# Sparse experts in a fused two-layer kernel: tokens sorted by expert in two halves, the first half's sorting placed inside the last attention iterations, and the order tables rewritten

## The chip, the cores and the metric

The kernel runs on one core of one Trainium2 chip. The metric is the device time of one execution in microseconds (us). A profiled execution also has a span: the time from its first to its last recorded instruction. TensorE is called PE, VectorE DVE, ScalarE ACT, GpSimd POOL; SyncE (SP) issues the DMAs.

## The reference, cut to what matters

Two layers run on 4 batches of 256 tokens with 128 channels (1,024 tokens) and a context of 512 rows for each batch. Layer 0 is cross-attention with 8 heads of 64 and a feed-forward with a quantized piecewise-linear GELU. Layer 1 is cross-attention with 16 heads of 8, with a small ReLU block, and then a mixture of 8 experts of which each token takes its best two:

```python
def _L1_ffn_ref(x, Wg, W1, W2, W3):
    t = x.reshape(-1, D)                      # 1024 x 128
    probs = jax.nn.softmax(t @ Wg, axis=-1)   # 8 experts
    top_v, top_i = jax.lax.top_k(probs, TOP_K)          # TOP_K = 2
    top_v = top_v / (jnp.sum(top_v, axis=-1, keepdims=True) + 1e-08)
    comb = jnp.zeros((T, E), dtype=t.dtype).at[jnp.arange(T)[:, None], top_i].add(top_v)
    out = jnp.zeros_like(t)
    for e in range(E):
        h = jax.nn.silu(t @ W1[e]) * (t @ W3[e])        # 128 -> 512
        out = out + comb[:, e:e + 1] * (h @ W2[e])      # 512 -> 128
    return out.reshape(Bb, Ll, D)
...
    x = x + _L1_ffn_ref(_layernorm(x, axis=-1), L1_ffn_Wg, L1_ffn_W1, L1_ffn_W2, L1_ffn_W3)
```

## The kernel before, in words

**Order of work.** One function, `schedule()`, writes a single list of steps, and each engine walks the same list and does its own share of each step (`for kind, *at in order`). The attention part of the list comes from eight iterations, one for each layer and batch (0 to 3 are layer 0, 4 to 7 are layer 1). Every step has a place inside its iteration, counted in heads; the places stand in the tables `PLACES` (a default for each layer) and `SHIFTED` (values for one iteration), and the list is sorted by them. The engines meet only in semaphores, so a wait on one engine holds back everything behind it in that engine's part of the list.

**Attention.** For each head PE computes scores twice: once for the row maxima (`maxima`, L468, reduced by DVE in L766) and once transposed (`scores`, L498), whose exponential ACT takes from PSUM (L1056). `attend` (L530 in layer 1) multiplies by the values. In layer 1 an iteration has 16 heads; maxima of the next batch are taken one iteration ahead, so iteration 7 needs none of its own. Layer 0's feed-forward and layer 1's projections of earlier batches stand between the heads. POOL splits the 24 expert weight blocks into a high and a low float16 part in iterations 4 to 7 (`split`, L1212 and L1213); SP loads them (`stage_in`, L1314).

**Experts.** After the last head the list has 2 halves x 8 experts x 4 chunks of 128 hidden units. A half is 512 tokens, and every expert is computed for all of them. For a chunk PE does six matmuls of 512 columns (`gate_up`, L653: up and gate, each as high x high, high x low and low x high), ACT takes the SiLU (L1122), DVE the product (L953), ACT and DVE split it into a high and a low part (L1129, L958). For each expert `down` (L670; `down_last`, L684, for the final one) does 48 matmuls of 128 columns, and DVE's `mix` (L968) adds each result to `x_sb` with the token's share `comb`, which is zero for the six experts that the token doesn't take. Shares come from `logits`, `route` (with an exponential written as a power on POOL, L1204), `shares`, `compare`, `rank` and `best`. The list `rest` puts those steps, and the last batch's projections, between the chunks. At the end SP writes each half of the output in one DMA (L1339).

**PSUM.** `p_misc` has four banks used in turn (`misc_take`, `misc_wait`, `misc_done`); in the expert part two of them hold the up product and the other two stay in turn. `p_sc` holds the gate product and `p_o` the down product.

Of the kernel before, what the change touches and what calls it, by code (L numbers as in the profile page):

```python
# [8 lines left out]
F16 = mybir.dt.float16  # L9
AX_X = mybir.AxisListType.X  # L10
# [20 lines left out]
VW = DH1 + 1  # L31

# [3 lines left out]
    0: {"max": (1.5, 1.0), "sum": 1.38, "av": (-0.38, 0.96), "f_ln": -0.65, "f_xn": 0.92, "f_xT": 1.2,  # L36
        "up0": (1.4, 0.13), "round": 1.57, "floor": 2.0, "nodes": 2.17, "slope": 3.0, "interp": 3.5, "ident": 3.7,
# [17 lines left out]
    (2, 'f_ln'): 0.02, (2, 'interp'): 3.48, (2, 'q1'): 5.66, (2, 'slope'): 2.71, (2, 'sum'): 2.35,  # L55
    (2, 'v0'): (3.6, 1.02), (3, 'av'): (-0.45, 0.96), (3, 'nodes'): 2.58, (3, 'oT'): (5.14, 0.71), (3, 'sT'): 3.68,
    (3, 'v1'): 5.23, (4, 'av'): (0.05, 1.0), (4, 'bounce'): 12.04, (4, 'down0'): 7.55, (4, 'f_ln'): 1.46,
    (4, 'f_xT'): 2.5, (4, 'f_xn'): 2.1, (4, 'floor'): 3.9, (4, 'ident'): 6.9, (4, 'interp'): 6.3,
    (4, 'nodes'): 4.19, (4, 'oT'): (5.0, 1.99), (4, 'round'): 3.55, (4, 'rows'): 2.08, (4, 'slope'): 5.5,
# [3 lines left out]


def schedule():
# [27 lines left out]
    for it in range(2 * B):  # L93
# [10 lines left out]
        if nxt:  # L104
            put(it, 1.7 if it == 0 else -0.01, "stack0" if nxt[0] == 0 else "stack1", nxt[1])
# [68 lines left out]
        if it == 2 * B - 1:  # L174
            put(it, 0, "split", 3 * E - 1)
            for i in range(2):
                tokens(lambda name, n, *what: step(name, *what, n=n), i, i)
            step("route", "route", 0)
# [4 lines left out]
    rest = {0: [("oT1", B - 1, 0)], 1: [("oT1", B - 1, 1)], 2: [("shares", 0)], 3: [("compare", 0)], 4: [("rank", 0)], 5: [("best", 0)],  # L183
            6: [("aT1", B - 1)], 8: [("h1", B - 1)], 10: [("y1", B - 1)]}
    for i, b in enumerate((2, 3)):
        for chunk, kind in ((11, "ln"), (13, "xn"), (15, "xT")):
            rest[chunk + 5 * i] = rest.get(chunk + 5 * i, []) + [(kind, "ex", b)]
        rest[17 + 5 * i] = [("logits", b)]
    rest.update({24: [("route", 1)], 28: [("shares", 1)], 30: [("compare", 1)], 34: [("rank", 1)], 36: [("best", 1)]})
    for n in range(2 * E):  # L190
        for f in range(FF):
            order.append(("gu", n, f))
            if n and f >= 2:
                order.extend([("dn", n - 1, 2 * (f - 2)), ("dn", n - 1, 2 * (f - 2) + 1)])
            order.append(("act", n, f))
            order.extend(rest.get(FF * n + f, []))

    order += [("dn_last", f) for f in range(FF - 1)] + [("act", 2 * E, 0), ("dn_last", FF - 1), ("mix", 2 * E - 1)]
# [28 lines left out]
def build(nc, t, out):  # L227
    ctx = ExitStack()
    with ctx:
# [39 lines left out]
        ew = [region[:, 8192 * i:8192 * (i + 1)].rearrange("p (s e n) -> p s e n", s=2, e=E) for i in range(3)]  # L269
# [15 lines left out]
        xh = qS[:, 0, 0:8, :].rearrange("p h n -> p (h n)").rearrange("p (s n) -> p s n", s=2)  # L285
        cmp_ = kS[:, 0, 0:4, :].rearrange("p h n -> p (h n)").bitcast(F32).rearrange("p (s t e f) -> p s t e f", s=2, t=B * T, e=E)
# [6 lines left out]
        euler = sb("euler", [P, 1])  # L293
# [23 lines left out]
        hh = probs[:, 2:6, :].bitcast(F16).rearrange("p (b s) (f n) -> p b s f n", b=2, f=FF)  # L317
# [5 lines left out]

        dk = nc.dram_tensor("k_scratch", (B, 3, P, C), F16).ap()
# [67 lines left out]
        def _(pe):  # L392
# [44 lines left out]
            def xt(kind, b):  # L437
                n = norms.index((kind, b))
                pe.wait_ge(ln_xn, n + 1)
                transposes(("xT", kind, b), [xn[:, n % 2, i, :] for i in range(T)])  # L440
# [259 lines left out]
        def _(dve):  # L700
# [271 lines left out]
            def activate(n, f):  # L972
# [3 lines left out]
                if k:  # L976
                    low(k - 1)
# [393 lines left out]
```

## Time and profile before

| | us |
|---|---|
| median of 3 runs (lowest, highest) | 501.96 (501.45, 503.52) |
| the profiled execution | 501.99 |
| its span | 500.3 |
| PE busy in the span | 436.3 (87%) |
| DVE busy | 367.7 (73%) |
| ACT busy | 266.2 (53%) |
| POOL busy | 176.6 (35%) |
| mean granted clock of TensorE | 0.939 of full speed |

Busy time of PE is modelled from the size of each matmul and includes overlap of matmuls that are in the pipe together, so a group of matmuls is costed below by the distance between the starts of groups, not by the duration of one. The share of busy time is a mean over stages with different limits, and the stages must be read one by one.

### The profile page before, as it was taken

The numbers are of one execution on the slowest core, as the hardware profiler recorded it, in microseconds if no ns is written. First come the engines' busy times: TensorE is split into PE (matmuls) and PEld (weight loads), VectorE is DVE, ScalarE is ACT, GpSimd is POOL, SyncE is SP. The second block draws the span as 40 slices with busy tenths as digits, with TensorE's granted clock in tenths as the row PEclk, the third lists the DMA queues.
The fourth block names the chain that finished last, engine by engine and source line by source line (L and its number), as shares of the span: only waits on it lengthen the run. The fifth ranks groups of instructions, "written<-read, shape, count | busy, mean of one in ns | idle before, by whom it ended". The sixth has DMA issues, their size and how long they took to land.

```text
span 500.3 us, 8970 instructions
## 1 busy us (share of the span) xinstructions
PE 436.3 (87%) x3344; PEld 248.6 (50%) x3344; DVE 367.7 (73%) x718; ACT 266.2 (53%) x504; POOL 176.6 (35%) x205
## 2 busy tenths in 40 slices
PE   8569498997789968977985899999989999999996
PEld 3315154564356436544542544545546665656555
DVE  6855354555875799869986999882298888987775
ACT  3515253653824552456567376678755646465553
POOL 4218935427463492752426035710400104000000
PEclk9958698998979979997998899999999999999999
DMA  6664408007102005321142015400000000000000
GB/s 165 151 150 95 94 2 189 1 1 173 49 1 64 2 0 139 94 72 55 54 128 84 2 48 144 115 2 1 2 0 1 1 3 1 1 21 2 1 1 22
DMA packets 31487, 26.70 MB, mean 53 GB/s; under 512 B 4717, under 2 KB 28461, under 8 KB 31149
## 3 DMA queue, kind: packets, MB, share of 16 engines
q1 hardware_dynamic: 31445, 26.13, 20.9%
q8 instruction: 27, 0.44, 0.4%
q14 instruction: 15, 0.12, 0.1%
HBM read 12.10 MB, written 2.88 MB: 30 GB/s over the span
## 4 chain that ended last, share of the span: by engine, by line
PE 59%; DVE 22%; ACT 7%; issue 4%; SPq 3%; DMA 2%; POOL 2%; DVEq 0%; ACTq 0%; POOLq 0%
PE p_o L670 7%; PE p_sc L498 7%; PE p_misc L653 7%; PE p_sc L653 6%; PE p_misc L468 6%; DVE mx L766 6%; PE p_o L530 5%; PE p_o L517 4%; PE p_misc L399 4%; SPq L1254 3%; DVE xn L729 2%; DVE probs L953 2%; PE p_misc L425 2%; PE p_misc L562 2%; ACT probs L1122 2%
## 5 line engine op out<-in xcount | busy, mean ns | idle before, releaser
L766 DVE TENSOR_REDUCE mx<-p_misc 128x1 f32<-128x512 f32 x192 | 122.3, 684 | 20.4 <-PE p_misc L468 18.8
L1056 ACT ACTIVATE probs<-p_sc 128x512 f32<-128x512 f32 x192 | 104.6, 596 | 57.2 <-PE p_sc L498 56.9
L1122 ACT ACTIVATE probs<-p_misc 128x512 f32<-128x512 f32 x64 | 38.1, 597 | 56.6 <-PE p_sc L653 56.6
L953 DVE TENSOR_TENSOR probs<-probs,p_sc 128x512 f32<-128x512 f32 x64 | 44.0, 687 | 26.5 <-ACT probs L1122 24.7
L653 PE MATMUL p_misc<-qS,region 128*128 128x512 f16 x192 | 52.0, 380 | 3.8 <-DVE probs L953 2.6
L653 PE MATMUL p_sc<-qS,region 128*128 128x512 f16 x192 | 51.9, 379 | 0.0
L468 PE MATMUL p_misc<-kS,qS 96*128 96x512 f16 x128 | 40.6, 395 | 8.1 <-DVE mx L766 4.1
L1195 POOL TENSOR_TENSOR psums<-probs 128x256 f32<-128x256 f32 x32 | 26.0, 812 | 58.6 <-PE p_o L524 56.1
L1153 POOL TENSOR_SCALAR veps<-meanvar 128x2 f32<-128x2 f32 x16 | 3.7, 230 | 121.7 <-DVE meanvar L718 121.3
L670 PEld LDWEIGHTS p_o<-region,probs 128*128 128x128 f16 x720 | 42.7, 98 | 7.1
L670 PE MATMUL p_o<-region,probs 128*128 128x128 f16 x720 | 45.1, 219 | 0.0
L517 PE MATMUL p_o<-probs,v 128*64 128x256 f32 x256 | 38.3, 423 | 7.0 <-ACT probs L1056 7.0
L498 PE MATMUL p_sc<-qS,kS 128*128 128x256 f16 x256 | 40.6, 278 | 4.2 <-ACT probs L1056 3.9
L958 DVE TENSOR_TENSOR probs<-probs 128x512 f16<-128x512 f32 x64 | 43.8, 684 | 0.0
L530 PE MATMUL p_o<-probs,v 128*32 128x256 f32 x512 | 41.0, 398 | 0.0
L1129 ACT CAST probs<-probs 128x512 f16<-128x512 f32 x64 | 39.1, 611 | 1.4 <-DVE probs L953 1.4
L498 PE MATMUL p_sc<-region 128*128 128x256 f16 x256 | 36.6, 290 | 0.9 <-DVE region L780 0.9
L498 PEld LDWEIGHTS p_sc<-qS,kS 128*128 128x128 f16 x256 | 23.4, 98 | 19.8 <-ACT probs L1056 8.0
L498 PEld LDWEIGHTS p_sc<-region 128*128 128x128 f16 x256 | 25.7, 103 | 12.6 <-issue 3.6
L1213 POOL TENSOR_TENSOR region<-v,region 128x512 f16<-128x512 f32 x24 | 30.3, 1264 | 1.9
L653 PEld LDWEIGHTS p_sc<-qS,region 128*128 128x128 f16 x192 | 18.8, 98 | 22.7
L517 PEld LDWEIGHTS p_o<-probs,v 128*64 128x64 f32 x256 | 16.8, 146 | 24.7 <-issue 12.7
(163 smaller groups left out, 678.6 us busy)
## 6 DMA issues: line engine op xcount, KB each, us to landing
region<-kx SPq DMA_DIRECT2D x24, 256.0 KB, 3.9
v<-in_L_ffn_W_dram SPq DMA_DIRECT2D x24, 256.0 KB, 2.7
region<-qx SPq DMA_DIRECT2D x24, 128.0 KB, 3.9
kS<-kS SPq DMA_DIRECT2D x1, 1664.0 KB
kS<-k_scratch SPq DMA_DIRECT2D x8, 192.0 KB
k_scratch<-kx SPq DMA_DIRECT2D x4, 256.0 KB, 2.2
qS<-q_scratch SPq DMA_DIRECT2D x8, 96.0 KB
probs<-in_ctx_dram SPq DMA_DIRECT2D x1, 576.0 KB, 6.2
```

The lines of the kernel that those rows point to most:

```text
L468: pe.matmul(ps, q[:, i * P:(i + 1) * P], k, start=True, stop=True).then_inc(full, 1)
L498: last = pe.matmul(p_sc[:, half, j * S:(j + 1) * S], k[:, kt * P:(kt + 1) * P], q, start=(i == 0), stop=(i == len(pairs) - 1))
L517: pe.matmul(p_o[64 * i:64 * i + 64, 0, m * S:(m + 1) * S], v0[:, b % 2, kt, h * DH0:(h + 1) * DH0], probs[:, h % 8, kt * S:(kt + 1) * S], ...
L530: last = pe.matmul(p_o[32 * j:32 * j + 32, n % 2, 0:S], v1[:, b % 2, c, h * VW:h * VW + 32], probs[:, h % 8, c * S:(c + 1) * S], start=(c ...
L653: last = pe.matmul(ps[:, f % 2, :], w[:, ws, e, f * P:(f + 1) * P], xh[:, xs, half * C:(half + 1) * C], start=(i == 0), stop=(i == 2))
L670: last = pe.matmul(p_o[:, n % 2, i * P:(i + 1) * P], hh[:, n % 2, hs, f, i * P:(i + 1) * P], ew[2][:, ws, e, f * P:(f + 1) * P], start=(at ...
L766: dve.tensor_reduce(mx[:, b % 2, i, h:h + 1], ps, AX_X, ALU.max).then_inc(free, 1)
L953: dve.tensor_tensor(hp[:, k % 2, :], sg[:, k % 2, :], p_sc[:, k % 2, :], ALU.mult).then_inc(hp_done, 1)
L958: dve.tensor_tensor(hh[:, n % 2, 1, f, :], hp[:, k % 2, :], hh[:, n % 2, 0, f, :], ALU.subtract).then_inc(hl_done, 1)
L1056: act.activation(probs[:, h % 8, half * 512:(half + 1) * 512], p_sc[:, half, :], ACT.Exp, scale=(DH0 if layer == 0 else DH1) ** -0.5).then ...
L1122: act.activation(sg[:, k % 2, :], p_misc[:, k % 2, :], ACT.Silu).then_inc(sg_done, 1)
L1129: act.copy(hh[:, last_n % 2, 0, last_f, :], hp[:, (k - 1) % 2, :]).then_inc(hh_done, 1)
```

## The change

The expert part no longer computes every expert for every token. The tokens of a half (512, each with two experts) are sorted by expert into slots of 128 rows. Each expert gets as many slots as its tokens need, rounded up; 15 slots (`SLOTS`) always suffice for a half, and all 15 are computed. For each half:

- DVE marks each token's two experts (`mask`, at the end of `rank`); PE counts them with eight small matmuls (`count`); DVE works out each token's two row numbers, each slot's expert and the shares (`place`).
- POOL writes the normalized tokens (`xe`) into DRAM at their row numbers with eight indirect DMAs (`send`); SP reads the sorted rows back with four DMAs (`fetch`); PE transposes them slot by slot and ACT and DVE split them (`taken_t`, steps `gT`).
- For each slot PE reads the slot's expert number into a register (`value_load`) and addresses the weights by it: six matmuls of 512 columns, four transposes of the product, then four matmuls of 256 and four of 128 columns. The result goes to DRAM (`keep`).
- POOL gathers each token's two results with eight indirect DMAs (`pick`), DVE adds them to `x_sb` (`mix`) and SP writes the output in four DMAs for a half (`store`).

The first half's sorting (`ex` steps of batches 0 and 1, `route` to `send`, `fetch`, `gT`) now has places in iterations 6 and 7; the second half's stands between slots 0 and 18 of the first (`REST`). Both DRAM buffers are filled with zeros once (`wipe`, 2 DMAs in iteration 3). The POOL power is replaced by an exponential on ACT. The tables `PLACES` and `SHIFTED` are rewritten for all iterations; among others, the maxima of the last batch now start at place 3.42 of iteration 6 and stand 1.26 apart (2.62 and 1.01 before), so that heads 10 to 15 fall into iteration 7.

```diff
+NT = B * T // 2
+SLOTS = 2 * NT + E - 1
+GROUPS = -(-SLOTS // 4)
...
+    (6, 'max'): (3.42, 1.26), (6, 'nodes'): 0.12, (6, 'oT'): (6.04, 2.2), (6, 'oT1'): (4.48, 0.24),
...
+REST = [(0.12, 'oT1', 3, 0), (0.72, 'oT1', 3, 1), (1.17, 'aT1', 3), (1.4, 'h1', 3), (1.55, 'y1', 3),
+        (1.93, 'ln', 'ex', 3), (2.05, 'xn', 'ex', 3), (3.06, 'xT', 'ex', 3), (3.27, 'logits', 3),
+        (3.29, 'route', 1), (3.51, 'shares', 1), (3.63, 'compare', 1), (3.68, 'rank', 1), (4.61, 'best', 1),
+        (4.79, 'count', 1), (4.84, 'place', 1), (5.44, 'send', 1), (8.85, 'fetch', 1), (11.76, 'gT', 1, 0),
+        (13.86, 'gT', 1, 1), (17.72, 'gT', 1, 2), (18.76, 'gT', 1, 3), (19.42, 'pick', 0), (20.61, 'mix', 0, 0),
+        (21.99, 'mix', 0, 1), (26.65, 'mix', 0, 2), (31.47, 'mix', 0, 3)]
...
+            for name in ("route", "shares", "compare", "rank", "best", "count", "place", "send", "fetch"):
+                step(name, name, 0)
+            for q in range(GROUPS):
+                step("gT", "gT", 0, q, n=q)
...
+    for k in range(2 * SLOTS):
+        placed += [(k, ("gu", k)), (k + 1.3, ("hT", k)), (k + 2.6, ("dn", k))]
+    placed += [(at, tuple(what)) for at, *what in REST]
+    order += [what for at, what in sorted(placed, key=lambda step: step[0])]
+    order += [("pick", 1)] + [("mix", 1, i) for i in range(NT)]
...
+            def gate_up(k):
+
+                half, j = k // SLOTS, k % SLOTS
+                if j == 0:
+                    pe.wait_ge(experts_set, half + 1)
+                misc_done(pe, ("gT", half, j // 4))
+                chosen[k] = pe.value_load(expert_id[0:1, half, j:j + 1], min_val=0, max_val=E - 1)
                 if k == 0:
+                    pe.wait_ge(stage_free, 3 * E)
...
                 for ps, w in ((p_misc, ew[0]), (p_sc, ew[1])):
                     for i, (ws, xs) in enumerate(((0, 0), (0, 1), (1, 0))):
+                        last = pe.matmul(ps[:, k % 2, :], takenT[half][:, xs, at], w[:, bass.ds(chosen[k], 1), ws, :].rearrange("p e n -> p (e n)"),
                                          start=(i == 0), stop=(i == 2))
                 last.then_inc(gu_full, 1)
...
+            def hidden_t(k):
+                pe.wait_ge(hp_done, k + 1)
...
+                for f in range(FF):
+                    last = pe.transpose(p_o[:, k % 2, f * P:(f + 1) * P], hp[:, k % 2, f * P:(f + 1) * P], ident[:, :])
+                last.then_inc(hT_full, 1)
+
+            def down(k):
+                pe.wait_ge(hl_done, k + 1)
+                ps, full = misc_take(pe, ("ym", k))
+                for f in range(FF):
+                    w = ew2[:, bass.ds(chosen[k], 1), f, :, :].rearrange("p e s n -> p (e s n)")
+                    pe.matmul(ps[:, 0:2 * P], hh[:, k % 2, 0, f * P:(f + 1) * P], w, start=(f == 0), stop=False)
+                for f in range(FF):
+                    w = ew2[:, bass.ds(chosen[k], 1), f, 0, :].rearrange("p e n -> p (e n)")
+                    last = pe.matmul(ps[:, 0:P], hh[:, k % 2, 1, f * P:(f + 1) * P], w, start=False, stop=(f == FF - 1))
+                last.then_inc(full, 1)
...
+            def send(half):
+
+                pool.wait_ge(slots_set, half + 1)
...
+                for i in range(NT):
+                    for s in range(2):
+                        pool.indirect_dma_start(d_in[half], bass.IndirectOffsetOnAxis(ap=slot_id[:, half, s, i:i + 1], axis=0),
+                                                xe[:, half * NT + i, :], None).then_inc(sent, 16)
...
+            def fetch(half):
+
+                sp.wait_ge(sent, 16 * 2 * NT * (half + 1))
...
+            def keep(k):
+                misc_done(sp, ("ym", k))
+                sp.dma_start(d_out[k // SLOTS].rearrange("(t p) n -> p t n", p=P)[:, k % SLOTS, :], y_sb[:, k % 4, :]).then_inc(y_kept[k % 4], 16)
```

## Rows read from the trace of the kernel before

**Rows 1.** Busy time of each engine by stretch; last columns: granted clock, DMA share, GB/s.
```profile
core 0: us, PE busy (x) PEld busy (x) DVE busy (x) ACT busy (x) POOL busy (x), PEclk, DMA share, GB/s
...
250.00:298.50 48.50, 39.51 (x314) 20.02 (x312) 41.94 (x76) 29.44 (x58) 16.27 (x18) 0.93 0.23 66
298.50:328.50 30.00, 30.00 (x276) 15.33 (x278) 26.22 (x48) 20.83 (x45) 17.83 (x20) 1.00 0.43 112
328.50:357.10 28.60, 27.65 (x268) 13.44 (x272) 13.67 (x35) 23.71 (x51) 1.87 (x4) 1.00 0.01 1
...
359.40:389.27 29.87, 27.26 (x207) 16.06 (x203) 23.47 (x62) 17.26 (x32) 4.71 (x3) 1.00 0.00 1
...
414.43:487.78 73.35, 72.30 (x648) 44.50 (x649) 59.49 (x130) 39.80 (x73) 5.42 (x1) 1.00 0.02 5
496.37:500.30 3.93, 0.01 (x1) 0.00 (x0) 1.13 (x4) 0.00 (x0) 0.00 (x0) 1.00 0.23 67
```

**Rows 2.** The chain that ended last: experts of the expert part, and its end.
```profile
414.43 0.82 PE p_misc L653 x3
...
422.58 0.82 PE p_misc L653 x3
...
430.73 0.82 PE p_misc L653 x3
...
495.53 0.86 PE p_o L684 x12
```

**Rows 3.** Groups of instructions from 380 us on: busy us, mean ns, idle before.
```profile
L958 DVE TENSOR_TENSOR probs<-probs 128x512 f16<-128x512 f32 x56 | 38.3, 684 | 0.0
...
L1129 ACT CAST probs<-probs 128x512 f16<-128x512 f32 x56 | 34.2, 611 | 0.4 <-DVE probs L953 0.4
L1122 ACT ACTIVATE probs<-p_misc 128x512 f32<-128x512 f32 x55 | 32.9, 597 | 50.9 <-PE p_sc L653 50.9
L968 DVE SCALAR_TENSOR_TENSOR x_sb<-p_o,comb,x_sb 128x128 f32<-128x128 f32 x60 | 16.8, 342 | 0.9 <-PE p_o L684 0.9
```

**Rows 4.** Timeline inside the expert part: weight loads that lead each group of matmuls.
```profile
423.03 0.53 PEld L653 LDWEIGHTS p_sc<-qS,region 128*128 128x128 f16 x3
...
423.67 1.54 PEld L670 LDWEIGHTS p_o<-region,probs 128*128 128x128 f16 x24
...
425.17 0.37 PEld L653 LDWEIGHTS p_misc<-qS,region 128*128 128x128 f16 x3
```

**Rows 5.** Timeline at the expert part's start: four float32 transposes, and ACT's table load.
```profile
360.50 0.57 PEld L399 LDWEIGHTS p_misc<-ident,osb 128*128 128x128 f32 x4
...
360.96 1.28 ACT L1122 ACT_TABLE_LOAD   x1 [1.05 <-PE p_sc L653]
361.04 0.21 PEld L653 LDWEIGHTS p_misc<-qS,region 128*128 128x128 f16 x2
```

**Rows 6.** Idle time by cause, 298.5 to 357 us: total, times, longest.
```profile
PEld p_misc L468 <- issue: 8.6, 21, 0.4
```

**Rows 7.** DMA issues: KB each and median us to landing.
```profile
v<-in_L_ffn_W_dram SPq DMA_DIRECT2D x24, 256.0 KB, 2.7
...
q_scratch<-qx SPq DMA_DIRECT2D x4, 64.0 KB, 2.3
```

**Rows 8.** Timeline: small routing operations of the second half on DVE.
```profile
423.04 0.18 DVE L910 TENSOR_REDUCE gs<-kS 128x4 f32<-128x32 f32 x1
...
423.25 0.18 DVE L911 RECIPROCAL gs<-gs 128x4 f32<-128x4 f32 x1
```

**Rows 9.** Groups of the attention stretch 298.5 to 328.5 us, on DVE and POOL.
```profile
L766 DVE TENSOR_REDUCE mx<-p_misc 128x1 f32<-128x512 f32 x33 | 21.0, 685 | 1.2 <-PE p_misc L468 0.9
...
L1213 POOL TENSOR_TENSOR region<-v,region 128x512 f16<-128x512 f32 x10 | 11.7, 1171 | 0.8
```

**Rows 10.** Line L1204, POOL's power: ns shortest, median, longest.
```profile
L1204 POOL TENSOR_TENSOR kS<-euler,kS x2: 5415/5417/5419, 358.2 to 415.4; 128x32 f32<-128x32 f32 x2
```

**Rows 11.** SP's own timeline: the last DMA's issue.
```profile
497.57 0.38 SPq L1339 DMA_DIRECT2D out_dram<-x_sb  x1
```

More of the change, by code:

```diff
@@ L48 @@
 }
 SHIFTED = {
[3 rows of a table removed]
[L55 to L59, printed above, removed]
[3 rows of a table removed]
+    (0, 'aT'): (3.66, 0.59), (0, 'av'): (-0.24, 0.54), (0, 'bounce'): 2.36, (0, 'down0'): 1.14, (0, 'f_ln'): -2.7,
@@ new lines @@
+    (4, 'h1'): 10.09, (4, 'ident'): 6.58, (4, 'interp'): 6.28, (4, 'k1'): 10.58, (4, 'logits'): (11.5, 1.48),
+    (4, 'max'): (2.47, 1.01), (4, 'nodes'): 4.55, (4, 'oT'): (4.72, 2.19), (4, 'oT1'): (18.12, 0.25),
+    (4, 'place'): 10.75, (4, 'q1'): 12.83, (4, 'q1_ln'): 7.71, (4, 'q1_xT'): 11.91, (4, 'q1_xn'): 9.6,
+    (4, 'rank'): 18.61, (4, 'round'): 3.87, (4, 'route'): 6.4, (4, 'rows'): 2.23, (4, 'sT'): 3.66,
+    (4, 'send'): 15.0, (4, 'shares'): 9.44, (4, 'slope'): 6.09, (4, 'split'): (-0.34, 1.66), (4, 'stack'): -3.82,
@@ new lines @@
+    (5, 'h1'): 8.78, (5, 'ident'): 5.1, (5, 'interp'): 5.07, (5, 'k1'): 10.36, (5, 'logits'): (4.91, 1.07),
+    (5, 'max'): (2.22, 1.01), (5, 'nodes'): 3.98, (5, 'oT'): (6.35, 2.05), (5, 'oT1'): (3.4, 1.16),
+    (5, 'place'): 16.09, (5, 'q1_ln'): 9.0, (5, 'q1_xT'): 11.0, (5, 'q1_xn'): 9.38, (5, 'rank'): 14.54,
+    (5, 'round'): 2.73, (5, 'route'): 14.46, (5, 'rows'): 2.32, (5, 'sT'): 2.47, (5, 'send'): 18.54,
+    (5, 'shares'): 1.65, (5, 'slope'): 4.93, (5, 'split'): (0.4, 2.09), (5, 'stack'): 1.01,
@@ new lines @@
+    (6, 'ident'): 12.55, (6, 'interp'): 4.47, (6, 'k1'): 6.09, (6, 'logits'): (10.56, 1.11),
+    (6, 'max'): (3.42, 1.26), (6, 'nodes'): 0.12, (6, 'oT'): (6.04, 2.2), (6, 'oT1'): (4.48, 0.24),
+    (6, 'place'): 15.07, (6, 'q1'): 8.33, (6, 'q1_ln'): 3.96, (6, 'q1_xT'): 7.11, (6, 'q1_xn'): 15.39,
+    (6, 'rank'): 12.93, (6, 'round'): -6.02, (6, 'route'): 11.78, (6, 'rows'): 2.61, (6, 'sT'): -5.38,
+    (6, 'send'): 15.21, (6, 'shares'): 12.4, (6, 'slope'): 5.77, (6, 'split'): (-1.14, 1.95), (6, 'stack'): -9.25,
@@ new lines @@
+    (7, 'h1'): 8.14, (7, 'ident'): -4.97, (7, 'interp'): 4.11, (7, 'k1'): 6.25, (7, 'logits'): (15.87, 0.41),
+    (7, 'max'): (9.36, 1.6), (7, 'nodes'): 4.83, (7, 'oT'): (0.36, 2.23), (7, 'oT1'): (4.08, 0.44),
+    (7, 'place'): 12.22, (7, 'q1'): 12.16, (7, 'q1_ln'): 10.64, (7, 'q1_xT'): 16.15, (7, 'q1_xn'): 1.87,
+    (7, 'rank'): 10.22, (7, 'round'): 2.49, (7, 'route'): 19.43, (7, 'rows'): 0.8, (7, 'sT'): 3.64,
+    (7, 'send'): 24.75, (7, 'shares'): 16.74, (7, 'slope'): 9.45, (7, 'split'): (-0.51, 1.6), (7, 'stack'): 4.54,
@@ L162, in schedule @@
                 step("v1", "init", 5)
+                step("wipe", "wipe")
                 step("zeros", "zeros")
@@ L175, in schedule @@
             put(it, 0, "split", 3 * E - 1)
+            tokens(lambda name, n, *what: step(name, *what, n=n), 2, 0)
+        if it == 2 * B - 2:
+            step("consts", "consts")
             for i in range(2):
                 tokens(lambda name, n, *what: step(name, *what, n=n), i, i)
-            step("route", "route", 0)
+            for name in ("route", "shares", "compare", "rank", "best", "count", "place", "send", "fetch"):
+                step(name, name, 0)
+            for q in range(GROUPS):
+                step("gT", "gT", 0, q, n=q)
     order = [what for _, _, _, what in sorted(placed)]
[L183 to L198, printed above, removed]
+    placed = []
+    for k in range(2 * SLOTS):
[3 more added lines that the diff above has]
+    order += [("pick", 1)] + [("mix", 1, i) for i in range(NT)]
     for b in range(B):
@@ L439, in xt @@
                 pe.wait_ge(ln_xn, n + 1)
-                transposes(("xT", kind, b), [xn[:, n % 2, i, :] for i in range(T)])
+                transposes(("xT", kind, b), [xn[:, n % 2, i, :] if kind != "ex" else xe[:, b * T + i, :] for i in range(T)])
             def queries0(b, i):
```

423 lines of the change are left out of this document (273 added, 150 removed), and 18 rows, old and new, of tables (PLACES, SHIFTED).

## Prediction

> **What bounds the kernel now.** I read the busy time by stretch first, to see which stages there are. The attention iterations 6 and 7 (298.5 to 328.5 and 328.5 to 357.1) and the expert part differ: in iteration 6 both PE (30.0 of 30.0 us) and DVE (26.2) are nearly full, in iteration 7 PE is full (27.7 of 28.6) but DVE is half idle (13.7), and in the expert part PE has 72.3 of 73.35 us [rows 1]. Then the chain that ended last: from 414.43 on it is PE alone, and one expert of one half takes 422.58 - 414.43 = 8.15 us, again and again [rows 2]. The groups of instructions show why nobody else matters there: ACT idles 50.9 us for PE before the SiLU, and no DVE operation is waited for in any amount [rows 3]. So the expert part is priced by PE's matmuls: its first group starts at 359.4 [rows 1], its last ends near 496.4 [rows 2], which is 137.0 us, of which 16 x 8.15 = 130.4 are experts and 6.6 the last batch's projections, norms and logits. After it stand 3.9 us of tail [rows 1].
>
> **What a slot costs on PE.** The starts of the groups give the price of a matmul: from 423.03 to 423.67 three of 512 columns pass, 0.214 us each; from 423.67 to 425.17 there are 24 of 128 columns, 0.0625 each [rows 4]. For 256 columns I take 0.107, half of the first. Four float32 transposes hold PE from 360.50 to 361.04, 0.54 us [rows 5]. A slot is 6 x 0.214 + 0.54 + 4 x 0.107 + 4 x 0.0625 = 2.50 us, and 30 of them 75.0 us, where the 16 experts cost 130.4. Beside it lie ACT's three operations (0.60 + 0.61 + about 0.3 for 128 columns) and DVE's three (0.69 + 0.68 + 0.34), 1.5 and 1.7 us [rows 3]: cover enough. The latencies fit the order too. From the end of a slot's `gu` to its product is 0.60 + 0.69 and some semaphores, about 1.5 us, while PE still has a whole slot (2.5) to do before that slot's `hT`; from `hT` to the split parts is about 1.5 us against 2.5 again.
>
> **Reading the expert's number.** Nothing in the trace loads a register from memory, or uses one as an address. Below it is nothing: `value_load` can run while earlier matmuls still stand in PE's queue. The nearest row from above is the pause of 8.6/21 = 0.41 us in which PE waits for its own issue [rows 6]; the farthest is a whole round trip through memory, 2.3 us [rows 7]. The matmuls of a slot and the waits ahead of its `hT` and `dn` let the queue run dry only in part, so I take 0.2 us for a slot, between nothing and the nearest row: 6.0 us.
>
> The Trainium skill (DMA: Bandwidth & Descriptors, Latency and other measured facts) gives a floor of about 600 ns for a `tensor_load`. No row here shows one; if nothing covered it, the sum would be 12 us longer by that page.
>
> **The rest of the expert part.** The old 6.6 us stay, less one batch's transposes and logits that move into iteration 7 (0.8), plus 15 transposes for the second half (15 x 0.135 = 2.0) and eight small matmuls of `count` (1.1): 8.9. The second half's routing is a chain on DVE, which is shorter in time now that slots are short: some 40 small operations, 0.21 us from start to start where they are linked [rows 8], come to 8.5 us, and the exponential on ACT forces the table out and in again, 1.28 us each time [rows 5]. All of it stands between slots 3 and 6, whose products, low parts and results need the same DVE. A slot leaves DVE about 0.8 us free, so with what is buffered I expect 6 us of idle PE there. The projections of the last batch (`oT1` to `logits`, a strict chain between slots 0 and 4) cost another 2, and the last slot's own latency, which nothing covers, 2. Sum: 75.0 + 6.0 + 8.9 + 6 + 2 + 2 = 99.9 us instead of 137.0.
>
> **The second half's data.** `send` stands at slot 5.4, `fetch` at 8.85, the first `gT` at 11.8, its use at 15. At 1.2 us for each of eight indirect DMAs (next paragraph), 2.3 to land and four reads of 256 KB at 2.7 [rows 7], the data is there about 9.6 + 2.3 + 4 = 16 us after `send`, at 2.7 us for a slot six slots later: in time. Queued behind the wait of `fetch` on SP are the writes `keep` from slot 7 on; four result buffers cover them until slot 11. Costed at nothing; if the indirect DMAs took double, it would be 5 to 10 us of idle PE. `pick` for the first half has ten slots' time before the last `mix`: hidden.
>
> **The tail.** Now after the last matmul: ACT and DVE 0.6, issue and landing of 64 KB 0.4 + 2.3 [rows 7, 11], eight gathers issued one after the other on POOL, the last landing 2.3, two DVE operations 0.7 [rows 3], and the output's DMA 0.4 + 2.3. POOL issues no DMA in this trace. From below a gather's issue costs what SP's costs, 0.38 us [rows 11]; from above what POOL's slowest operation costs, 5.4 us [rows 10]. POOL must work for 128 rows, so I take its ordinary 128-row operation, 1.17 us [rows 9]: 9.4 us. The tail is 0.6 + 2.7 + 9.4 + 2.3 + 0.7 + 2.7 = 18.4 instead of 3.9 us. The bounds make it 12 or 52.
>
> **Attention.** Iteration 6 loses six heads' maxima, 12 x 0.685 = 8.2 us of DVE [rows 9], and gets two norms (2.7) and the first half's routing with `place` (about 10.8 with its waits): 26.2 - 8.2 + 13.5 = 31.5 in a stretch of 30.0, so DVE becomes the longer one by 1.5 to 2. Iteration 7 gets the maxima (12 x 0.25 = 3 us of PE), `gT` of the first half (2.0) and one norm in place of two (-0.8): about 3 more, on a PE that is full; DVE has room for its 8.2. `send` and `fetch` of the first half lie beside iteration 7. The 2 MB of `wipe` go out in iteration 3, where SP has little to do. The rewritten places of iterations 0 to 5 keep every matmul and reduction. They can give or cost some us through waits, since iteration 5 takes 48.5 us with PE busy for 39.5 and DVE for 41.9 [rows 1]: I take nothing, with 6 either way. Attention: +5.
>
> **Sum.** 359.4 + 5 + 99.9 + 18.4 = 482.7, and with the 1.7 us that the profiled execution (501.99) has beyond its span 484.4. That execution equals the median of 501.96, so the forecast is 484.5 us, 3.5% less.
>
> **Rivals.** (a) PE's queue runs dry at each slot: the number's load and the addresses of 14 matmuls made from a register are not covered. For it speaks that the queue can only be ahead by the slack of the waits, about 1 us; against it, that PE's pauses here never exceed 0.41. It ends the gain where a slot costs 17.4/30 = 0.58 us more than in my sum, that is 0.8 in all; at 1.2 the time is 484.5 + 30 = 514.5. (b) Neither reading nor issuing costs much, and the rewritten places tighten iterations 4 and 5: -6, -4, -4 gives about 470. (c) Indirect DMAs at 2.5 us or more: the tail grows by 10.6, the second half comes late (+5), `gT` of the first half makes PE wait in iteration 7 (+3): about 503. (d) The routing chain of either half costs more than its sum, because each of its waits holds DVE's and then PE's queue: +10, 494. (e) The transposes cool PE. The granted clock is 1.00 where PE is full and 0.93 in iteration 5, where it is busy for 39.5 of 48.5 us [rows 1]; at 0.93 the slots cost 5 us more: 490.
>
> On (e) the Trainium skill (TensorE: Matmul & The Clock Gate, Part 4: PE-mode transpose) says that transpose mode doesn't count as PE being busy in the same way. By that rule the 0.54 us of each slot would speak for a lower clock; the trace has no stretch with such a mix.
>
> **Chances.** My forecast with its own range of 477 to 493, which holds (d) in part and (e): 0.55. (b) 0.18. (a) 0.13. (c) 0.07. (d) beyond 493: 0.07. A change within 0.5% (499.5 to 504.5) can't be told from none, more can. Faster by more than that: nearly all of the forecast, (b) and (d), and a third of (a) and (c), 0.86; the same 0.04; slower 0.10. The range leaves a tenth on either side: 465 to 503, down to (b) with a cheap tail, up to where (a) and (c) begin to decide.
>
> **What would show it.** Right: `gate_up` starts at a steady distance near 2.7 us, the last matmul ends near 464 and a tail of 18 us follows in which only POOL and DMAs act; iterations 6 and 7 end near 364. Wrong: idle time of PE put down to "issue" at each slot (a), ACT and DVE waiting for `gate_up` while PE waits for nothing; POOL issues further apart than 1.2 us (c); PE waiting for DVE for over 6 us between slots 3 and 6 (d); a granted clock under 1.00 (e); the expert part starting before 359 (b).

## The result: 4.3% faster, by a forecast in which two errors cancelled

The changed kernel takes 482.9 us where the kernel before took 502.6 in the same sitting. That is the median of four executions, of which a disturbed one of 2,002.7 us counts in no comparison; the other three took 481.2, 481.5 and 484.4. The ratio is 0.9574, interval 0.9531 to 0.9616. Forecast was 484.5. The profiled execution took 481.5 us, with a span of 479.4.

The start of each attention iteration (it) can be read on ACT, by its first exponential; the first SiLU belongs to slot 0 (before: to the first chunk of the first expert). The lengths in us:

| | it 0 | it 1 | it 2 to 5 | it 6 | it 7 to first SiLU | first to last SiLU |
|---|---|---|---|---|---|---|
| before | 39.4 | 38.6 | 188.1 | 28.8 | 29.3 | 129.7 |
| after | 32.1 | 33.2 | 186.8 | 35.7 | 38.1 | 94.2 |

So 12.7 us come from iterations 0 and 1, 1.3 from 2 to 5; 15.7 are lost in 6 and 7; the expert part gives 35.5; and the tail costs 13. The stretches of after that answer to [rows 1] (iterations 6 and 7; four pieces of the expert part; the tail):

```profile
core 0: us, PE busy (x) PEld busy (x) DVE busy (x) ACT busy (x) POOL busy (x), PEclk, DMA share, GB/s
...
289.60:326.00 36.40, 33.28 (x291) 17.09 (x289) 30.68 (x83) 21.85 (x48) 14.51 (x18) 0.95 0.28 74
326.00:361.05 35.05, 30.73 (x280) 14.33 (x278) 16.36 (x45) 22.01 (x46) 10.86 (x12) 0.95 0.15 45
361.05:382.75 21.70, 15.30 (x110) 10.12 (x107) 12.68 (x41) 11.62 (x21) 0.93 (x2) 1.00 0.02 7
382.75:402.07 19.32, 15.23 (x90) 9.00 (x91) 12.07 (x40) 6.85 (x15) 7.78 (x8) 0.91 0.14 45
402.07:423.40 21.33, 21.33 (x160) 15.06 (x161) 13.58 (x29) 12.46 (x27) 0.03 (x1) 1.00 0.25 72
423.40:441.00 17.60, 13.04 (x80) 7.58 (x79) 8.39 (x18) 5.80 (x14) 7.57 (x8) 0.92 0.21 57
...
461.00:479.40 18.40, 0.93 (x10) 0.61 (x8) 4.41 (x13) 0.53 (x2) 7.54 (x8) 0.62 0.20 57
```

The reader is to see that PE is full in only one of the pieces, 402.07 to 423.40, and that the piece behind it, made of the same kind of slots, has 4.6 us without PE and a lower clock. The two pieces in which PE idles on ACT and DVE without their being busy are 382.75 to 402.07 and 423.40 to 441.00, and in both POOL has its eight indirect DMAs.

The chain that ended last, which answers to [rows 2]: one slot, then the tail.

```profile
454.40 0.65 PE p_misc L781 x3
455.05 0.65 PE p_sc L781 x3
455.69 0.44 PE p_o L792 x4
456.13 0.44 PE p_misc L800 x4
456.57 0.22 PE p_misc L803 x4
456.79 0.65 PE p_misc L781 x3
...
463.17 1.52 DMA slots_out<-probs
...
465.42 0.94 POOL probs L1368
466.36 0.30 issue
466.66 0.94 POOL probs L1368
...
474.15 2.50 DMA probs<-slots_out,kx
```

A slot is 456.79 - 454.40 = 2.39 us, and PE waits for nobody in it. A gather takes 0.94 us on POOL and 0.30 pass to the next: 1.25 us each.

The number of the slot's expert is read on PE's queue. The line of the `value_load` (ns shortest, median, longest):

```profile
L768 PEldq TENSOR_LOAD <-kx x30: 297/302/484, 359.8 to 455.8; - x30
L768 PEldq FUSED_REGOPS  x30: 151/151/165, 360.3 to 456.2; - x30
```

It takes 0.30 + 0.15 us and lies wholly beside earlier matmuls: no group of PE in a steady slot has idle time ahead of it.

What had not been foreseen stands in PE's and ACT's timelines beside POOL's burst of gathers (`pick` 0; the number in brackets is the idle time ahead of the instruction):

```profile
427.45 0.39 PE L803 MATMUL p_misc<-region,probs 128*128 x4
```
```profile
427.65 0.60 ACT L1268 ACTIVATE probs<-p_misc 128x512 f32<-128x512 f32 x1 [1.69 <-PE p_sc L781]
430.51 0.58 ACT L1274 CAST probs<-p_o 128x512 f16<-128x512 f32 x1 [2.27 <-PE p_o L792]
434.80 0.27 ACT L1280 COPY probs<-p_misc 128x128 f32<-128x128 f32 x1 [3.71 <-remote]
```
```profile
423.37 0.98 POOL L1368 DMA_INDIRECT probs<-slots_out,kx  x1 [26.32 <-DMA slots_out<-probs]
...
432.16 0.94 POOL L1368 DMA_INDIRECT probs<-slots_out,kx  x1 [0.30 <-issue]
```

ACT's copy at 434.80 is that of slot 17. It needs the four matmuls from 427.45 on, whose end the trace puts at 427.84, yet it starts 7.0 us after that, the last 3.71 of them with ACT idle; the releaser is given as "remote", no engine of the trace. In a steady slot ACT starts 0.02 to 0.04 us behind PE's end. DVE and PE have gaps too ("issue" 2.28 us on PE at 431.96), but theirs follow from ACT's: DVE starts at 431.13, 0.04 us behind ACT's end (430.51 + 0.58), and PE at 431.96, 0.14 behind DVE's (431.13 + 0.69). So in the chain of a slot it is only PE's result that comes late, on its way to ACT. The same picture stands beside both sends: ACT idles 3.81 us up to 337.62 in iteration 7 (for matmuls that end at 333.54), and DVE 4.66 up to 339.16 for transposes that PE does from 333.38 on; ACT idles 1.59 up to 394.99 and 3.04 up to 398.62 in slots 5 and 6. Inside these gaps and the one of 3.71 us the trace has DMA packets of POOL's queue (`software_dynamic`) alone, none of the queues of kind `instruction`.

### The profile page after: what moved, and what is told of

It is laid out like the page before. It is cut to its first block, busy times and chain, and to the rows that moved or that the text cites. A ratio compares the mean times of both kernels' runs of the same rounds, so it can differ in the third digit from the quotient of the medians.

```text
span 479.4 us, 8292 instructions
## 1 busy us (share of the span) xinstructions
PE 389.9 (81%) x2778; PEld 222.9 (47%) x2778; DVE 334.5 (70%) x676; ACT 242.7 (51%) x474; POOL 196.0 (41%) x252
## 4 chain that ended last, share of the span: by engine, by line
PE 51%; DVE 25%; issue 7%; ACT 6%; SPq 4%; DMA 3%; POOL 2%; another core or an unknown queue 2%; POOLq 0%; DVEq 0%; ACTq 0%
PE p_sc L606 7%; DVE mx L879 6%; PE p_misc L576 6%; PE p_o L638 5%; PE p_o L625 4%; PE p_misc L507 4%; PE p_misc L781 3%; PE p_sc L781 3%; SPq L1430 3%; PE p_o L792 3%; PE p_misc L533 2%; PE p_misc L800 2%; PE p_misc L680 2%; DVE xn L849 2%
## 5 line engine op out<-in xcount | busy, mean ns | idle before, releaser
L1368 POOL DMA_INDIRECT probs<-slots_out,kx x16 | 15.1, 946 | 62.9 <-DMA slots_out<-probs 58.6
L1101 DVE TENSOR_TENSOR probs<-probs,p_sc 128x512 f32<-128x512 f32 x30 | 20.6, 685 | 25.7 <-ACT probs L1268 21.4
L625 PE MATMUL p_o<-probs,v 128*64 128x256 f32 x256 | 34.7, 391 | 4.3 <-ACT probs L1190 4.3
L606 PE MATMUL p_sc<-region 128*128 128x256 f16 x256 | 34.3, 278 | 0.9 <-DVE region L893 0.9
L1268 ACT ACTIVATE probs<-p_misc 128x512 f32<-128x512 f32 x30 | 18.0, 601 | 31.2 <-PE p_sc L781 31.2
L1358 POOL DMA_INDIRECT slots_in<-qx,kx x16 | 15.9, 994 | 31.0 <-issue 17.2
L576 PE MATMUL p_misc<-region 128*128 128x512 f16 x64 | 21.9, 413 | 6.8 <-DVE kx L868 2.0
L1348 POOL TENSOR_TENSOR psums<-psums,probs 128x256 f32<-128x256 f32 x32 | 26.3, 821 | 2.5
L1347 POOL TENSOR_TENSOR psums<-psums,probs 128x256 f32<-128x256 f32 x32 | 25.1, 785 | 2.5
L1105 DVE TENSOR_TENSOR probs<-p_o,probs 128x512 f16<-128x512 f32 x30 | 20.5, 685 | 5.9 <-ACT probs L1274 3.6
L576 PEld LDWEIGHTS p_misc<-kS,qS 96*128 96x128 f16 x128 | 11.5, 101 | 25.0 <-DVE mx L879 15.6
```

The source lines that it names most:

```text
L576: pe.matmul(ps, q[:, i * P:(i + 1) * P], k, start=True, stop=True).then_inc(full, 1)
L606: last = pe.matmul(p_sc[:, half, j * S:(j + 1) * S], k[:, kt * P:(kt + 1) * P], q, start=(i == 0), stop=(i == len(pairs) - 1))
L625: pe.matmul(p_o[64 * i:64 * i + 64, 0, m * S:(m + 1) * S], v0[:, b % 2, kt, h * DH0:(h + 1) * DH0], probs[:, h % 8, kt * S:(kt + 1) * S], ...
L1101: dve.tensor_tensor(hp[:, k % 2, :], sg[:, k % 2, :], p_sc[:, k % 2, :], ALU.mult).then_inc(hp_done, 1)
L1347: link(pool.tensor_tensor(psums[:, h % 4, :], psums[:, h % 4, :], tiles[2], ALU.add))
L1348: pool.tensor_tensor(psums[:, h % 4, :], psums[:, h % 4, :], tiles[3], ALU.add).then_inc(sums_set, 1)
```

## The experiments

Kernels from different sittings are compared by their ratio to the kernel before of the same sitting; the changed kernel's is 0.9574. A difference of 0.01 in it is 5 us.

**1. The places of iterations 0 and 1 as before**

```diff
-    (0, 'k0'): (5.1, 0.6), (0, 'stack'): 0.59, (1, 'k0'): (3.76, 0.56), ...
+    (0, 'k0'): (3.3, 0.6), (0, 'stack'): 1.7,  (1, 'k0'): (2.01, 0.61), ...
```

> The changed kernel, but the steps of attention iterations 0 and 1 stand at the places that they had before the change. Theory 1 (the rewritten places of iterations 0 and 1 alone gave the 12.7 us by which these two got shorter, 78.5 to 65.7 us): the kernel takes about 12.7 us more, 495 to 496, the two iterations take 39.9 and 38.6 us again, and PE waits about 6.7 us at the third chunk of the keys of batch 2. Theory 2 (they were slow before for another reason, such as the state of DMA queues or of the clock): less than 4 us of difference.

Measured: 499.0 us, 0.9913 (0.9876 to 0.995), 16 to 17 more than the changed kernel. Iterations 0 and 1 take 39.5 and 38.6 us. The longest waits between 37 and 77 us:

```profile
DVE kx L1116 <- ACT kx L1406: 14.7, 4, 8.7
...
ACT kx L1406 <- DMA region<-qx: 8.5, 1, 8.5
...
PE p_misc L781 <- DVE kx L1116: 6.7, 1, 6.7
```

ACT waits 8.5 us for the DMA that stacks keys in SBUF, DVE's part of those keys stands behind ACT, and PE's next keys behind DVE. (Lines are those of this kernel.) In the changed kernel 0.9 us of that wait for the DMA is left. Theory 1 holds; the 3 us beyond its 12.7 lie in iterations 2 to 5, which take 189.8 us against 186.8, and are not explained.

**2. The new places of iterations 0 and 1 alone, in the kernel before**

```diff
-            put(it, 1.7 if it == 0 else -0.01, "stack0" ...
+            put(it, {0: 0.59, 1: -4.96}.get(it, -0.01), "stack0" ...
```
and the changed kernel's values of `SHIFTED` for iterations 0 and 1.

> The kernel before the change, with nothing changed but the places of iterations 0 and 1, which are those of the changed kernel (the first stacking of iteration 0 at 0.59 and that of iteration 1 at its start, too). Theory 1 (these places alone gave the 12.7 us, and need nothing else of the change): 12 to 16 us less than the kernel before, 486 to 490. Theory 2 (they work only with the later tables): iterations 2 and 3 get longer by what 0 and 1 get shorter, and the gain is under 6 us.

Measured: 490.9 us, 0.9744 (0.9711 to 0.9777), 12.6 less than the kernel before. Iterations 0 and 1 take 32.3 and 32.8. So the places of two iterations, without any sorting, give 12.6 of the 20 us by which the change is faster.

**3. A fixed expert for each slot**

```diff
-                chosen[k] = pe.value_load(expert_id[0:1, half, j:j + 1], min_val=0, max_val=E - 1)
+                chosen[k] = j // 2
```

> The changed kernel, but slot j of a half always uses the weights of expert j // 2: PE reads no number from memory into a register and builds no address from one. It leaves out that the expert follows the sorting, so the numbers computed are other ones; the matmuls and their order are the same. Theory 1 (reading the number lies wholly beside earlier matmuls): a steady slot stays at 2.39 us, the time is the same within 1 us. Theory 2 (it costs the 0.2 us for a slot that the prediction took): 2.2 us a slot, 6 us less. Theory 3 (PE's queue runs dry at each slot): 0.5 us or more for a slot, at least 15 us less.

The kernel leaves out that the expert follows from the sorting; its numbers are other ones. Measured: 484.5 us, 0.9617 (0.9582 to 0.9652), not told apart from the changed kernel; a steady slot stays at 2.39 us. Reading the number is free. Rival (a) is out, and so is the 0.2 us for a slot in the sum.

**4. The first half's sorting behind the attention part**

```diff
-            for name in ("route", "shares", "compare", "rank", "best", "count", "place", "send", "fetch"):
-                step(name, name, 0)
-            for q in range(GROUPS):
-                step("gT", "gT", 0, q, n=q)
+            step("route", "route", 0)
...
+    order += [(name, 0) for name in ("shares", "compare", "rank", "best", "count", "place", "send", "fetch")]
+    order += [("gT", 0, q) for q in range(GROUPS)]
```

> The changed kernel, but of the first half's sorting only route stays in iteration 6; shares, compare, rank, best, count, place, send, fetch and the 15 transposes stand behind the last attention step, ahead of slot 0. Theory 1 (the chain is worth its own latency, and the steps in iterations 6 and 7 cost less than that): DVE's chain of some 8 us, eight indirect DMAs of 1.25 us, their landing and the reads back, about 9.5, and the first transposes, 1, all uncovered: 26 to 30 us, less 3 to 8 us which iterations 6 and 7 get back, so 500 to 508 us. Theory 2 (the steps in iterations 6 and 7 are what made these 15.7 us longer, nearly as dear as the bare chain): iterations 6 and 7 get 12 us shorter, and the time is 490 to 498.

Measured: 499.8 us, 0.9927 (0.9888 to 0.9966). From the last exponential to the first SiLU pass 34.9 us instead of 5.6, so 29.3 us of chain stand bare (PE waits 17.6 of them for the rows from DRAM). Iteration 6 is 4.1 us shorter (31.6), iteration 7 up to its last exponential 7.0 (25.5 instead of 32.5). Each theory had one half of it: the bare chain is worth 29, and hiding it costs 11.

**5. Indirect DMAs in pairs**

```diff
                 for i in range(NT):
+                    if i and half == 0:
+                        pool.wait_ge(sc_free[1], head_number(1, B - 1, 2 * i))
+                    if i and half == 1:
+                        pool.wait_ge(hp_done, 5 + i)
                     for s in range(2):
...
+                    if i and half == 0:
+                        pool.wait_ge(hp_done, 18 + i)
```
The last two lines are in `pick`; places in `REST` move as the text says.

> The changed kernel, but the eight indirect DMAs of send (both halves) and of the first half's pick go out in four pairs, each pair held back by a wait on POOL: two attention heads apart for the first send, one slot apart for the second send and for pick. The second half's fetch stands 2 slots later, its first two transposes 1 slot later, and the first two mix steps 1 slot later. Theory 1 (the stalls of ACT with its inputs ready, 3.8 us at 337.6, 1.6 and 3.0 at 395 to 402, 2.3 and 3.7 at 430.5 to 438.5, come from a long burst of indirect DMAs): with pairs they shrink or vanish, 6 to 12 us less. Theory 2 (they come with each indirect DMA, however far apart): the same time lost in smaller pieces, within 2 us of the changed kernel. Theory 3 (they have nothing to do with POOL's DMAs): the stalls stay where they are, and the time stays.

Measured: 477.1 us, 0.9472 (0.9446 to 0.9499), some 5 us less than the changed kernel. Many of the waits were already met, so that up to six DMAs still went out 1.26 us apart. Gaps were left (3.37 us on ACT in the second send, 3.16 beside four gathers in a row). This was not yet a clean test, and gave too little to tell theory 1 from 2. The next four separate burst, count and kind.

**6. Eight more gathers, in one burst at slot 12**

```diff
+            def extra(k, n):
+                pool.wait_ge(hp_done, k)
+                pool.indirect_dma_start(picks[1][:, n % 2, n // 2, :], None, d_in[0],
+                                        bass.IndirectOffsetOnAxis(ap=slot_id[:, 0, n % 2, n // 2:n // 2 + 1], axis=0)).then_inc(extra_done, 16)
...
+    placed += [(at, tuple(what)) for at, *what in [(12.1, 'extra', 12, n) for n in range(8)]]
```

> The changed kernel with eight more indirect DMAs on POOL in one burst, from slot 12 of the first half on, where slots run at a steady 2.39 us. They gather rows that nobody uses into a tile that is free until the end. Theory 1 (a burst of eight indirect DMAs stops ACT, DVE and PE for 4 to 6 us, whatever is computed beside it): a gap of 4 to 6 us opens some 5 us after the burst's start and the time is 4 to 6 us more. Theory 2 (the three gaps of the changed kernel have causes of their own, and fall together with the bursts by chance): the slots stay at 2.39 us and the time stays within 1 us.

**7. The same eight, one for each slot** (places `11.1 + n`, waits `11 + n`)

> As the kernel with the extra burst, but the eight extra gathers go out one for each slot, from slot 11 to slot 18, each held back by a wait for that slot's product. Theory 1a (what stops the engines is several indirect DMAs close together): no gap, and the time of the changed kernel within 1 us. Theory 1b (each indirect DMA takes its part, about 0.6 us): eight small gaps, and 4 to 6 us more, as in the burst. Theory 2 (no connection): no gap in either of the two kernels.

**8. Eight plain DMAs of 64 KB from POOL in the burst's place**

```diff
-                pool.indirect_dma_start(picks[1][:, n % 2, n // 2, :], None, d_in[0], ...
+                pool.dma_start(picks[1][:, n % 2, n // 2, :], d_in[0].rearrange("(t p) n -> p t n", p=P)[:, n, :]).then_inc(extra_done, 16)
```

> As the kernel with the extra burst, but the eight extra transfers are plain DMAs of 64 KB that POOL issues, one after the other, to the same tile; POOL works out no row numbers. Theory 1 (the indirect form is what stops the engines): no gap, and the time of the changed kernel within 1 us. Theory 3 (any burst of transfers on this queue or into this tile does it): the same 4 to 6 us as the burst of indirect DMAs.

**9. The same eight gathers in groups of two, three and three** (slots 11, 13 and 16)

> The changed kernel with the same eight extra gathers, now two together at slot 11, three together at slot 13 and three together at slot 16, 1.25 us apart inside a group. The four together of the spaced kernel's pick stood beside a gap of 3.2 us, single ones beside none. Theory A (a gap opens as soon as indirect DMAs stand less than some 2 us apart): gaps of 1 to 2 us at slots 12, 14 and 17, 4 us in all. Theory B (it takes more than three in a row): the slots 11 to 18 stay at 2.39 us (2.83 with a gT), as with single ones.

| | median us | ratio (interval) | distances of the SiLUs of slots 12 to 16 |
|---|---|---|---|
| burst of eight | 491.2 | 0.9743 (0.9671, 0.9815) | 5.91 4.99 4.31 3.36 |
| one for each slot | 488.0 | 0.9686 (0.9605, 0.9768) | 2.39 2.84 2.39 2.39 |
| eight plain | 484.7 | 0.9598 (0.9520, 0.9676) | 2.39 2.83 2.39 2.40 |
| two, three, three | 484.2 | 0.9612 (0.9549, 0.9675) | 2.39 3.49 1.73 2.97 |

(2.39 is a slot, 2.83 a slot with a `gT`.) Beside the burst, PE, ACT and DVE:

```profile
418.32 0.81 PE L783 MATMUL p_sc<-region,kS 128*128 x3
```
```profile
418.39 0.27 ACT L1282 COPY probs<-p_misc 128x128 f32<-128x128 f32 x1 [0.54 <-PE p_misc L805]
422.69 0.60 ACT L1270 ACTIVATE probs<-p_misc 128x512 f32<-128x512 f32 x1 [4.04 <-PE p_sc L783]
425.54 0.59 ACT L1276 CAST probs<-p_o 128x512 f16<-128x512 f32 x1 [2.25 <-PE p_o L794]
```
```profile
423.32 0.69 DVE L1103 TENSOR_TENSOR probs<-probs,p_sc 128x512 f32<-128x512 f32 x1 [4.34 <-issue]
```

The SiLU at 422.69 needs the matmuls from 418.32 on, which end at 419.13 by the trace: ACT gets them 3.56 us late. DVE's product follows that SiLU within 0.03 us.

With one for each slot, POOL and ACT:

```profile
411.23 0.95 POOL L1365 DMA_INDIRECT probs<-slots_in,kx  x1 [1.41 <-DVE probs L1103]
414.07 0.94 POOL L1365 DMA_INDIRECT probs<-slots_in,kx  x1 [1.89 <-DVE probs L1103]
416.46 0.94 POOL L1365 DMA_INDIRECT probs<-slots_in,kx  x1 [1.45 <-DVE probs L1103]
```
```profile
412.48 0.60 ACT L1270 ACTIVATE probs<-p_misc 128x512 f32<-128x512 f32 x1 [0.71 <-PE p_sc L783]
...
414.87 0.60 ACT L1270 ACTIVATE probs<-p_misc 128x512 f32<-128x512 f32 x1 [1.03 <-PE p_sc L783]
```

The four slots beside the burst take 18.56 us, beside the plain DMAs 10.01: a burst of eight costs 8.5 us there, in that trace. (The burst's profiled execution took 497.5 us, the other three 489.3 to 492.7, and those three are on average 6.7 us above the four with plain DMAs.) One for each slot opens no gap in slots 11 to 18. Its time misses what was expected all the same (within 1 us of the changed kernel; the ratios say 5 to 6 more), and its median is 3 us above the plain DMAs'. That fits its last one, which goes out at 426.47, right ahead of `pick`'s eight: nine in a row, and slot 18 to 19 takes 9.54 us. A pair opens none. Three in a row at slot 13 delay one SiLU by 0.66 us (3.49 where a slot with a `gT` takes 2.83), the next distance is as much shorter, but the one behind is 0.57 longer: a small price and not nothing, so that neither theory A nor B is met. The last three cost nothing more. So it is the indirect form, and several close together: theory 1 with 1a holds; 1b, 2 and 3 fall.

**10. The chain between slots 0 and 15 spread out** (`REST` alone is changed)

> The changed kernel with the chain between slots 0 and 15 spread out: aT1 1.5, h1 2.1, y1 2.7, ln 2.9, xn 3.5, xT 4.1, logits 4.7, route 4.8, shares 5.0, compare 5.4, rank 5.8, best 6.5, count 6.7, place 6.8, send 7.4, fetch 10.6, first two gT 13.6 and 14.4 (1.17 to 13.86 before). Nothing else changes. Theory 1 (the 12 us that slots 1 to 6 lose beside their 2.39 us each are waits of PE's and DVE's in-order queues for this chain's latencies): 4 to 7 us less. Theory 2 (they are the chain's own busy time on DVE and ACT, which has to be done somewhere): within 2 us of the changed kernel. Rival: the second half's rows now come too late, and what slots 1 to 6 give back is lost ahead of slot 15: the same or longer.

Measured: 483.1 us, 0.9602 (0.9523 to 0.9681), the same. First to last SiLU 91.6 us against 94.2. The two longest waits, 2.8 and 1.6 us, became 1.9 and 0.4, but slots 2 and 3 now stand 4.30 us apart instead of 2.39, and the burst of the send falls later. Theory 2 in the time, but for 2.6 us of the profiled execution.

**11. No two indirect DMAs closer than a slot or a head**

```diff
                     for s in range(2):
+                        if half == 0:
+                            pool.wait_ge(sc_free[1], head_number(1, B - 1, 2 * i + s))
+                        else:
+                            pool.wait_ge(hp_done, 6 + 2 * i + s)
                         pool.indirect_dma_start(d_in[half], ...
...
+                        if half == 0:
+                            pool.wait_ge(hp_done, 19 + 2 * i + s)
                         pool.indirect_dma_start(picks[half][:, s, i, :], ...
```

> The changed kernel, but no two of the indirect DMAs of send and of the first half's pick go out closer than a slot or a head: each waits on POOL for one more attention head (first send) or for one more slot's product (second send, pick 0). The second half's fetch stands at 13.0, its gT at 14.7, 17.0, 20.0 and 22.0, the mix steps at 22.5, 24.5, 26.65 and 28.6, the first half's gT half a head later. Theory (bursts cost 4 to 9 us each, single indirect DMAs nothing): iteration 7 gets 3 to 4 us shorter, the steady 2.39 us hold from slot 7 on but for 1 to 4 us of waiting ahead of slot 15, since the last row goes out 9 us later: 466 to 474 us. Rival (what counts is the spacing of the expert part's other steps, as in the spaced pairs): 475 to 480.

The places of `fetch`, `gT` and `mix` move along, as the text says. Measured: 472.2 us (470.3 to 475.0), 0.9392 (0.9364 to 0.9419). By the ratios that is 9 us less than the changed kernel, and 6.1% less than the kernel before; the profiled executions, 470.3 and 481.5, lie 11.2 apart. Iteration 7 takes 33.7 us instead of 38.1; the first five of the first send still went out 1.3 to 1.5 us apart, with no gap beside them. First to last SiLU takes 86.6 instead of 94.2. Its stretches from slot 7 to slot 14 and from there to the end of the matmuls:

```profile
385.00:409.40 24.40, 21.94 (x164) 15.11 (x162) 15.01 (x31) 12.64 (x28) 7.78 (x8) 1.00 0.29 87
409.40:449.00 39.60, 38.31 (x287) 26.80 (x287) 26.45 (x57) 21.50 (x49) 7.59 (x8) 1.00 0.17 47
```

PE is now full beside `pick`, at a granted clock of 1.00. The price stands ahead of slot 15, on PE:

```profile
407.45 0.66 PE L530 MATMUL p_misc<-ident,kS 128*128 128x128 f32 x4 [0.96 <-DMA kS<-slots_in]
410.34 0.82 PE L804 MATMUL p_misc<-region,probs 128*128 x3 [2.24 <-DVE probs L1118]
```

The sorted rows come 3 us late, and the distance of slots 14 and 15 is 6.43 us, 4.0 above a slot. So the two bursts had cost 94.2 - 86.6 + 4.0 = 11.6 us in the expert part and the first one 4.4 in iteration 7. That is what these two traces give; the steps that moved along may have a part in it, and the clean price of a burst is that of experiments 6 to 9. What is shown of their effect: in this kernel ACT starts at most 0.07 us behind PE's end in every slot from slot 5 on.

**12. As 11, with the last batch's maxima where they stood before**

```diff
-    (6, 'max'): (3.42, 1.26),
+    (6, 'max'): (2.62, 1.01),
```

> As the kernel with single indirect DMAs, but the maxima of the last batch stand where they stood before the change, from place 2.62 of iteration 6 on and 1.01 apart. Theory 1 (by the prediction's sum, DVE is the longer one in iteration 6 and moving six maxima out of it was needed): iteration 6 gets 6 to 8 us longer, iteration 7 some 3 us shorter, 3 to 5 us more in all. Theory 2 (the move of the maxima made iteration 7 longer by what it saved in iteration 6): within 2 us of the kernel with single indirect DMAs.

Measured: 477.5 us, 0.9471 (0.9438 to 0.9505), 4 to 5 more than kernel 11. Iteration 6 takes 41.2 us instead of 35.8; iteration 7 gets no shorter (35.3 and 33.7), where theory 1 had 3 us less, and slot 15 waits 1.9 longer. Theory 1 holds in its time and in iteration 6: DVE had to be relieved there. Theory 2 falls.

## Point by point

- **Slot on PE** (2.50, and 0.2 for the number): 2.39 and nothing. 30 x 2.39 = 71.7 us, where the sum had 81. The term of the transposes was 0.54 and is 0.44; the reading of the number lies beside matmuls, as the bound from below had it.
- **The rest of the expert part** (8.9 + 6 + 2 + 2 = 18.9): it goes from 361.05 to the last matmul's end at 462.5, 101.5 us against 99.9. Less the slots that leaves 29.8, of which the bursts are 11.6. The other 18.2 are near the 18.9 that were forecast, as a sum; its terms are not told apart. The waits behind them, over slots 0 to 7, stand in this order:

```profile
PE p_misc L748 <- DVE kx L1044: 2.8, 1, 2.8
PE p_o L792 <- DVE probs L1101: 1.8, 2, 1.1
PE p_misc L507 <- DVE a L991: 1.6, 1, 1.6
```

- **The step that failed** is "at 1.2 us for each of eight indirect DMAs" with `pick` "hidden". The size was right (1.25), and the second half's data was in time. But the DMAs were priced as work of POOL alone, and `pick` as costing nothing. Eight in a row hold back PE's results, and with them ACT, DVE and PE, 16.0 us in all over the three bursts that lie beside matmuls (11.6 + 4.4).
- **The tail** (18.4): 16.9, from 462.5 to 479.4. From the first gather's start to the last one's landing pass 11.2 us (465.42 to 476.65) where the sum had 9.4 + 2.3; the write of the last slot took 1.5 instead of 0.4 + 2.3.
- **Attention, iterations 0 to 5** (nothing, 6 either way): 14.0 us less. That was the other failed step. The rows read for it were those of iteration 5; the wait that the new places remove stands in iteration 0, from which no row was taken; there it alone is larger than the 6 us allowed.
- **Attention, iteration 6** (+2): +6.9. The sum over DVE was about right (31.5 forecast, 30.68 measured), but DVE is not full: the stretch is 36.4 long. A chain of short linked operations on an in-order queue also costs the waits between them; experiment 4 puts 4.1 of the 6.9 on the steps from `shares` to `place`.
- **Attention, iteration 7** (+3): +8.8, of which 4.4 are the burst and 4.4 the rest.
- **The sum.** Start of the experts 364.4 forecast, 361.05 measured: -14.0 and +15.7 where 0 and +5 were expected. The total is right within 3 us because the tables gave what the bursts and the sorting took, and that is luck: the two errors have nothing to do with each other.
- **Rivals.** (a) is refuted by experiment 3. (b) was half right: the tables do give 14 us, 12.7 of them in iterations 0 and 1 instead of 4 and 5. (c) is out, an indirect DMA takes 1.25 us. (d) shows in part, in the first half's chain: iteration 6 is 4.9 us above its sum. The second half's shows nothing beyond its place in the sum. (e) fell as it was put: the clock is 1.00 in the slots of 402.07 to 423.40, with 0.44 us of transposes in each 2.39. In the expert part it is lower only in stretches in which PE idled, or behind such (0.91 and 0.92), and it returns to 1.00 beside `pick` once the burst is gone (experiment 11). By the rule of the Trainium skill that the prediction cited (TensorE: Matmul & The Clock Gate, Part 4: PE-mode transpose) the transposes would speak for a lower clock; in these slots the trace shows none.
- **`tensor_load`.** The Trainium skill (DMA: Bandwidth & Descriptors, Latency and other measured facts) gives a floor of about 600 ns; here it took 302 ns in the median, and none of it on the path.

## What to carry to other kernels

Price an asynchronous operation by what it does to the other engines as well as to its own: indirect DMAs one or two at a time cost nothing here, three in a row 0.6 us, eight in a row 4 to 8.5 us of everybody. A rewritten order table is a change of its own: read the waits of every stretch that it touches, the first ones too. And where a forecast is a sum, compare it term by term even when the total is right.

## What the runs showed of the hardware

- A burst of eight indirect DMAs from POOL (128 rows of 512 bytes each, 1.25 us apart) costs ACT, DVE and PE 8.5 us when it lies beside steady slots (6.7 by the mean times of experiments 6 and 8, without the burst's slowest execution). The first gap opens 3 to 6 us after the burst's start. What comes late is PE's result to ACT: 3.56 us behind the end of the matmuls in experiment 6 and up to 7.0 in the changed kernel, against 0.02 to 0.04 in a steady slot, while DVE follows ACT within 0.14 beside the same burst. In iteration 7 DVE, too, gets PE's result late. The ends of matmuls are modelled, so the trace does not say whether PE's signal or the matmul itself is late. Eight plain DMAs of the same bytes, 0.55 us apart, do nothing of the kind. What POOL's burst and PE's results share here stays open: no trace shows it, and no run tried it. Five in a row in iteration 7 opened no gap (experiment 11), four gathers did (experiment 5), so the number alone does not decide.
- Nothing speaks for the gaps being a product of the profiling: the changed kernel's profiled execution (481.5 us) is not longer than the others (481.2 and 484.4), and with the bursts taken apart all six executions are faster (470.3 to 475.0).
- A register load on PE takes 302 ns and, with 151 ns for the address, hides under the matmuls queued before it.
